# Attention kernel on one core: weighted sums issued for two key tiles at a time, eight half tiles of probabilities kept

## What is computed

```
q, k, v = heads of x @ Wqk.T + b, x @ Wv.T + b      # 8 heads, 8 wide
scores  = einsum('bhqd,bhkd->bhqk', q, k)           # 2048 x 2048 per head
attn    = softmax(scores, axis=-1) / 8
out     = einsum('bhsl,bhlv->bhsv', attn, v) @ Wo.T + bo
```

## Time and profile before

| what | value |
|---|---|
| median of 3 runs | 2071.76 us (2070.28 to 2081.23) |
| span of the profiled execution | 2078.6 us |
| attention, from the first exponential to the last copy | 206.0 to 562.4 us |
| PE busy over the whole span | 1674.6 us, 81% |
| mean granted clock of PE | 0.813 |

### The profile page before, as it was taken

One profiled execution on the slowest core, in us unless ns is written; L12 is line 12 of the kernel. 1 busy time (PEld: TensorE's weight loads), 2 busy tenths in 40 slices (PEclk: granted clock), 3 DMA queues, 4 the chain that ended last, 5 costly groups with the idle time before them and its releaser, 6 DMA issues. The chain is left out here.

```text
span 2078.6 us, 24318 instructions
## 1 busy us (share of the span) xinstructions
PE 1674.6 (81%) x8224; PEld 892.4 (43%) x8224; DVE 1421.7 (68%) x2408; ACT 1094.6 (53%) x2004; POOL 1042.8 (50%) x585
## 2 busy tenths in 40 slices
PE   6882999999779984969598796978969788555578
PEld 2520222332156443746265563745637465222332
DVE  3263888888074112058999989899998999998131
ACT  2330666666721112266757576585766857643064
POOL 0000000000044004048998998999989999998102
PEclk9765899999965995969597895978969698556799
DMA  5333000000093436243454444445344544542301
GB/s 211 144 56 45 1 4 2 3 3 3 6 309 149 137 111 225 83 107 77 106 113 95 106 98 105 107 103 123 80 99 116 112 97 91 118 101 56 117 21 61
DMA packets 151261, 192.37 MB, mean 93 GB/s; under 512 B 18245, under 2 KB 123461, under 8 KB 149344
## 3 DMA queue, kind: packets, MB, share of 16 engines
q1 hardware_dynamic: 143250, 168.00, 32.4%
q0 software_dynamic: 4576, 16.79, 2.3%
q10 hardware_dynamic: 3312, 6.03, 0.8%
HBM read 142.60 MB, written 48.18 MB: 92 GB/s over the span
## 5 line engine op out<-in xcount | busy, mean ns | idle before, releaser
L1740 DVE TENSOR_TENSOR_SCAN ssm_scan<-ssm_psum,ssm_state,ssm_scan 128x256 f32<-128x256 f32 x1024 | 683.6, 729 | 34.9 <-ACT ssm_psum L1616 34.2
L1323 POOL TENSOR_TENSOR ssm_scan<-ssm_scan,ssm_bc 128x1024 f32<-128x1024 f32 x256 | 600.4, 2362 | 50.2 <-DVE ssm_state L1743 50.2
L1616 ACT ACTIVATE ssm_psum<-ssm_rep,ssm_a 128x256 f32<-128x256 f32 x1024 | 433.4, 468 | 182.6 <-DVE ssm_scan L1740 182.0
L1447 PE MATMUL ssm_psum<-ssm_scan,ssm_select 128*32 128x256 f32 x2048 | 205.9, 484 | 209.3 <-POOL ssm_scan L1323 206.8
L659 DVE TENSOR_REDUCE att_rowmax<-att_psum 128x1 f32<-128x512 f32 x448 | 278.1, 683 | 72.6 <-PE att_psum L554 72.6
L632 ACT ACTIVATE att_probs<-att_psum 128x1024 f32<-128x1024 f32 x256 | 248.4, 1021 | 150.3 <-PE att_psum L572 150.0
L1308 POOL TENSOR_TENSOR ssm_scan<-ssm_rep,ssm_bc 128x1024 f32<-128x1024 f32 x128 | 301.8, 2358 | 40.6 <-PE ssm_psum L1447 30.1
L554 PE MATMUL att_psum<-att_k,att_q 72*128 72x512 bf16 x448 | 159.3, 397 | 38.6 <-DMA att_k<-parts 37.5
L1447 PEld LDWEIGHTS ssm_psum<-ssm_scan,ssm_select 128*32 128x32 f32 x2048 | 46.0, 120 | 327.5 <-POOL ssm_scan L1323 225.3
L532 POOL COPY att_v<-v_tokens 128x128 f32<-128x128 f32 x8 | 2.3, 294 | 362.8 <-ACT att_out L626 362.8
L1725 DVE TENSOR_TENSOR ssm_scan<-ssm_rep,ssm_psum 128x1024 f32<-128x1024 f32 x128 | 155.4, 1214 | 7.5 <-PE ssm_psum L1447 4.4
(11 more groups left out here) (230 smaller groups left out, 2029.5 us busy)
## 6 DMA issues: line engine op xcount, KB each, us to landing
ssm_rep<-drive_rows SPq DMA_DIRECT2D x256, 256.0 KB, 4.6
qkv_wmod<-in_wmod SPq DMA_DIRECT2D x8, 1536.0 KB, 12.1
moe_we<-in_we SPq DMA_DIRECT2D x8, 1024.0 KB, 14.5
ssm_bc<-bc_rows SPq DMA_DIRECT2D x32, 256.0 KB, 5.3
drive_rows<-ssm_delta SPq DMA_DIRECT2D x64, 128.0 KB, 1.7
drive_rows<-ssm_du SPq DMA_DIRECT2D x64, 128.0 KB, 1.8
sorted_rows<-moe_zeros SPq DMA_DIRECT2D x1, 5888.0 KB, 19.2
moe_sorted<-sorted_rows SPq DMA_DIRECT2D x23, 256.0 KB, 3.4
```

Of the source, the lines that this page charges most:

```text
L1323: nc.gpsimd.tensor_tensor(scan[:, Q % RING], scan[:, Q % RING], bc[:, c % 2, 1, gr, :].unsqueeze(1).to_broadcast([P, J, SW]), ALU.mult).th ...
L1447: last = nc.tensor.matmul(ps_y[t % 2][32 * j:32 * j + 32, :], select[:], scan[:, Q % RING, j, :], start=(gr == 0), stop=False)
L1616: nc.scalar.activation(ps_decay[n % HALF_BANKS][:, i], rep[:, s % 2, 0, j, :], ACT.Exp, scale=amat[:, t, gr, j:j + 1]).then_inc(decay_done, 1)
L1740: nc.vector.tensor_tensor_scan(scan[:, Q % RING, j, :], ps_decay[(2 * Q + j // 2) % HALF_BANKS][:, j % 2], scan[:, Q % RING, j, :], state[ ...
```

## The change

The weighted sums of two neighbouring key tiles are issued as one run of eight float32 matmul instructions (16 records), behind the second `scores` of every even key tile from 2 on, for the two tiles before it. Those of tiles 14 and 15 of a head are issued at key tile 0 of the next head, or at the very end. The ring of probabilities has eight slots instead of four, 16 KB more in each partition of SBUF. The number of instructions is the same; nothing changes on the other engines but the thresholds that ScalarE waits for.

```diff
-    RING = 4
+    RING = 8
...
+            def weighted_pair(hh, b, kt):
+                weighted(hh, b, kt)
+                weighted(hh, b, kt + 1)
...
                     if kt == 0 and before is not None:
-                        weighted(*before)
-                    if kt > 0:
-                        weighted(hh, b, kt - 1)
+                        weighted_pair(*before)
+                    if kt > 0 and kt % 2 == 0:
+                        weighted_pair(hh, b, kt - 2)
                     max_scores(2)
-                return hh, b, KTILES - 1
+                return hh, b, KTILES - 2
...
-            weighted(*before)
+            weighted_pair(*before)
```

## The result

The changed kernel takes 2107.26 us (median of 5, 2090.77 to 2111.27) where the one before took 2075.36 (median of 5, 2070.28 to 2081.23): ratio 1.0148, interval 1.0107 to 1.0188. It is slower, by 32 us in the medians. Two later comparisons, each beside fresh runs of the kernel before, gave 2102.08 against 2070.82 (ratio 1.0157, 1.0121 to 1.0194) and 2107.0 against 2081.09 (1.0115, 1.0068 to 1.0163): 31 and 26 us.

What follows compares the result with a forecast made beforehand. PE was taken to bound attention, VectorE and ScalarE close behind; 6.8 + 4.3 + 8.2 + 0.35 - 0.5 = +19.2 us on the median 2071.8 gave 2091.0. Its own range was 2085 to 2098, the 8-in-10 range 2078 to 2107.

Steps and rivals of the forecast that it cites:

- The bound and its loops: Attention: PE leads with VectorE and ScalarE close behind; pairs make PE wait on three maxima banks and two score bank pairs.
- all three places: Pairs with maxima 5.80 us against 5.67 (+6.8), ends of heads' maxima (+4.3), part without maxima 4.99 against 4.17 (+8.2).
- the ends of maxima: Where a head's maxima end, the next pair comes 1.06 us late instead of 0.34, six times: +4.3 us.
- The second sum for 0.85: Weighted sums on PE: a second in a row adds 0.85 us, so a pair blocks PE for 1.85.
- The rival in which it costs 1.00: Each sum of a pair costs its full 1.00 us on PE: +9.3 us more, 2100.3; chance 0.05.
- The last pair: At attention's very end, the second sum adds 0.85 us behind the last exponential, less some 0.5: +0.35 us.
- Head 0's -0.5: Head 0's first tiles, PE at half clock and the bound: two pairs save some 0.5 us in all.
- The ring costs nothing: The eight-slot ring of probabilities never makes ScalarE wait, and a longer ring leaves the stage before head 0 untouched: 0.
- the likeliest case: The main forecast: attention's waits make the kernel +19.2 us slower, 2091.0 us; chance 0.65.
- The rival of the clock: PE's waits let its clock fall to half in the part without maxima: up to +22.6 us, 2113.6; chance 0.12.
- The rival on the other side: PE alone sets the time in attention: -12.0 us with maxima, -2.9 in the last part, 2057; chance 0.08.

Runs made afterwards that it cites:

- e3: Changed kernel with pairs of sums only while row maxima are left, single sums after; copies 11.9 us over the kernel before, ratio 1.0095.
- e4: Changed kernel with single sums while maxima are left, pairs only after them; copies 7.5 us over the kernel before, ratio 1.0086.
- e11: Kernel before once more, no edit, for a second profile; copies 303.4 us apart, its one run took 2092.78 us.
- e2: Kernel before with only the ring of probabilities doubled from four to eight, sums single; copies 0.1 us over before, ratio 1.0058.
- e1: Changed kernel again, no edit, for a second profile; copies 27.8 us over the kernel before, clock fell in 5 pairs, ratio 1.0157.
- e10: Changed kernel a third time, no edit, beside fresh runs of before; copies 26.1 us over before, clock fell in 4 pairs, ratio 1.0115.
- e12: Changed kernel with unread matmuls filling PE's waits in the part without maxima; copies 19.5 us over before, clock 1.00, ratio 1.01.
- e6: Kernel before (single sums) with VectorE's maxima over 256 of 512 columns; copies 1.7 us under before, ratio 0.9992.
- e8: Kernel before with 29 chained copies of ps_o on ScalarE ahead of the last head's final copy; copies 18.0 us over before, ratio 1.0111.
- e5: Changed kernel with VectorE's maxima over 256 of 512 columns; two tiles 5.68 us, copies 11.9 us over before, ratio 1.0042.

## Why the prediction was right, point by point

*The bound and its loops.* Right in kind at all three places, and close in size. With maxima 5.85 us was measured where 5.80 was forecast: the matmul that waits starts 4.23 - 3.48 = 0.75 after the start of the maximum that frees it, not 0.70. Over 52 pairs that term is 52 x 0.18 = 9.4, not 6.8. At the ends of maxima it is 1.03 - 0.34 = 0.69 each, 4.1 in place of 4.3. Without maxima it is 5.03 in place of 4.99. e3 and e4 give the halves alone: 11.9 and 7.5 from copy to copy.

*The second sum for 0.85.* Right: 1.92 for 16 records, as in the earlier trace rows. The rival in which it costs 1.00 is dead, and with it, for these matmuls, the reading by which loads of weights to equal row groups can't run beside matmuls in flight.

*The last pair.* Wrong, for +0.35. The pair at the very end is no pair: the first sum ran at 577.62 while the last exponentials were still under way, and only the second waited, at 579.28, as before, where the two stood at 559.02 and 560.68. So this term is 0. The pair ahead of it costs 0.85 like a full period, which makes ten in all, as reckoned: 9 x 0.86 + 0.85 = 8.6, where the prediction had 8.2 + 0.35.

*Head 0's -0.5.* It can't be read: from the first exponential to the first copy it was 52.5 us before and 53.2 after, but 57.7 in e11.

*The ring costs nothing.* Right in attention (e2, 0.1 us).

*Sum.* Forecast +19.2 us for attention, measured +20.2 over the same stage in the first pair of profiles (+19.5 from copy to copy, which leaves out head 0). The stated time, 2091.0, is that of the profiled execution (2090.77), but this was partly luck: its stages behind attention were 8.3 us shorter than before's. The median, 2107.26, is 16.3 us over it: outside the forecast's own range of 2085 to 2098, and 0.3 past the upper end of the wide one, 2107. Of the 16.3, 3.6 are the base, since the sum was added to a median of three runs, 2071.76, and five runs of the same kernel give 2075.36. The other 12.7 are the change's cost, 31.9 between the medians where 19.2 was forecast. Attention with the clock at 1.00 accounts for 1.0 of them; the others lie in the next two points, which the likeliest case had at nothing. So the direction, the places and the waits were right, and the size of the total was not.

*The rival of the clock.* It had 0.12 and deserved more. Among its signs of being wrong the prediction named a clock in attention that leaves 1.00 after 225 us; the first profile kept it at 1.00, and e1 and e10 didn't. The fall isn't the alternative to the forecast but comes on top of it in part of the executions: three of five profiles with pairs in the last part. Its size was put at 2.26 a pair, with all of PE's work at half clock; it is 1.65, as only the sums run slow and the clock is back for the scores. That the waits of the pair let the clock fall is the likely reading, not a shown one: in attention every fall behind head 0's start came with pairs, and e12 tried it with a single profile. The average of the three profiles of the changed kernel is 5.0 us (0, 8.3, 6.6).

*What stays open.* The whole of attention and the clock make 20.2 + 5 = 25, and the medians are 32, 31 and 26 apart. In the profiles the rest isn't in attention. Behind attention they vary from 1507.6 to 1523.4 us for identical instructions, before's two being 1516.2 and 1522.0, after's three 1507.9, 1511.7 and 1523.4. Most of it is one place, the gate matmuls of the expert stage (line 865 before). From the start of the first to that of the last they take 45.5 and 50.1 us in the two profiles of before, and 37.5, 38.2 and 50.1 in the three of after. Here are 20 us of the kernel before, from 52 us behind the end of attention, columns as in the earlier trace rows:

```profile
614.00:634.00 20.00, 20.00 (x80) 16.58 (x79) 13.14 (x29) 4.68 (x12) 12.06 (x10) 0.50 1.04 385
```

And the same piece of work in the first profile of the changed kernel:

```profile
633.00:653.00 20.00, 18.75 (x95) 17.61 (x95) 15.09 (x29) 5.66 (x14) 15.25 (x12) 0.62 1.04 385
```

The clock was at half throughout in the one and for part of the time only in the other (0.50 and 0.62); why it falls earlier or later was not tried. In these profiles the stages behind attention are not longer with the pair, so I find no sign that the change costs anything there. One rival wasn't tested: that the longer ring costs a few us outside attention. For it speaks that e2's medians are 12 us apart with equal attention, while the two kernels with a ring of four, e6 and e8, come within 2 us of what their attention shows. Against it, the ten profiles with a ring of eight took 1507.6 to 1523.4 us behind attention and the four with a ring of four 1515.5 to 1522.0, and e12's median is 3 us less over before than its copies are. The medians of before itself were 2075.36, 2070.82, 2077.97 and 2081.09 us in the four sets of runs, so the first two comparisons may hold a few us of chance.

*The rival on the other side* (PE alone, 2057) is dead for a better reason than the one given. e5 takes VectorE's loop away, and the pair still only reaches parity with maxima, by ScalarE's loop.

## What to carry to other kernels

Issuing like work in longer runs saved the changes between kinds, here 0.24 us a pair on PE, but it starved the engines that PE feeds through a fixed number of banks. Before batching, walk each ring of buffers once around: length of the run + refill + the consumer's operations up to the one that frees the next buffer; the longest such loop is the new period, and when one is mended the next lies just under it (5.85, then 5.68, with PE's own 5.44 never reached). Deepening the buffer that isn't the tight one (the ring of probabilities) bought nothing in attention (e2). And one profile of a kernel can mislead: the first one here showed neither the falls of the clock nor the median total.

## What the runs showed of the hardware

- Two groups of four float32 matmuls on 32 columns take 1.92 us back to back, one 1.06 to 1.07, at the higher clock; four pairs of e10 whose sums ran at the lower one for all or most of the time took 3.31 to 3.59.
- With PE waiting 0.69 and 0.31 us in each 5.03, the granted clock fell in some executions and held in others, for the same instructions: 0, 5 and 4 slow pairs in three profiles of one kernel. When it fell in e10, it was 0.51 in the sums, 1.00 in the scores behind them and 0.52 in the next sums. The Trainium skill, "TensorE: Matmul & The Clock Gate", Part 1, says that the default is the throttled state, that activity releases it, and that the moment of release varies from run to run; the traces agree in so far as the state differs between executions of one kernel.
- A maximum over 128 x 256 in PSUM takes 0.42 us in the median (e5, e6), one over 128 x 512 0.68 (all other runs).
